# Decay factors by a VectorE scan over rows read back from memory, in place of triangle products and exponentials

## The reference, cut to what matters

```
dt_p = softplus(dt + dt_bias)
A    = -exp(A_log)
dA   = exp(dt_p * A)                  # one factor per sequence, step and head
dtx  = dt_p[..., None] * x
def step(state, inp):
    dA_t, dtx_t, B_t, C_t = inp
    state = state * dA_t[..., None, None] + dtx_t[..., None] * B_t[:, :, None, :]
    y_t = einsum('bhpn,bhn->bhp', state, C_t)
    return (state, y_t)
y = ys + x * D
y = group_norm(y) * norm_weight * silu(gate)
out = y @ out_proj_w.T
```

## Time and profile before

| | |
|---|---|
| median of three runs | 1590.43 us (1589.69 to 1590.87) |
| the profiled execution | 1589.33 us, span 1587.3 us |
| TensorE busy | 1557.8 us, 98% of the span |
| VectorE, ScalarE, GpSimd busy | 1049.1, 852.2, 786.5 us |
| mean granted TensorE clock | 0.996 of full |
| DMA | 80.54 MB, mean 51 GB/s |

### The profile page before, as it was taken

The page is one execution under the profiler, slowest core; times in us unless marked ns, Lnnn a source line. Parts: engine busy times, 40 slices in busy tenths (PEclk is TensorE's granted clock), DMA queues, the critical chain, the costliest instruction groups (busy, mean ns, idle before and its releaser), DMA issues. The chain is left out here.

```text
span 1587.3 us, 32373 instructions
## 1 busy us (share of the span) xinstructions
PE 1557.8 (98%) x12991; PEld 1273.6 (80%) x12991; DVE 1049.1 (66%) x1689; ACT 852.2 (54%) x1420; POOL 786.5 (50%) x747
## 2 busy tenths in 40 slices
PE   8999999999999999999999999999999999999997
PEld 6778888888888888888887888888888888888687
DVE  5877666565657766576877656667565656666566
ACT  4654556555555556555465555555555554545542
POOL 3564545545364554545354463654545463643506
PEclk9999999999999999999999999999999999999999
DMA  6120101111120201111012111202011111103212
GB/s 200 54 60 20 55 21 54 41 41 54 34 61 8 61 28 54 41 41 54 1 55 94 41 54 35 60 8 61 28 54 41 41 54 34 42 20 90 86 41 107
DMA packets 49525, 80.54 MB, mean 51 GB/s; under 512 B 4897, under 2 KB 13601, under 8 KB 49377
## 3 DMA queue, kind: packets, MB, share of 16 engines
q1 hardware_dynamic: 49376, 78.48, 16.0%
HBM read 70.07 MB, written 8.39 MB: 49 GB/s over the span
## 5 line engine op out<-in xcount | busy, mean ns | idle before, releaser
L434 PE MATMUL PS<-xh,wh 128*128 128x512 f32 x1280 | 520.6, 407 | 0.6 <-DVE xl L954 0.6
L434 PE MATMUL PS<-xh,wl 128*128 128x512 f32 x1280 | 500.6, 391 | 0.0
L434 PE MATMUL PS<-xl,wh 128*128 128x512 f32 x1280 | 499.4, 390 | 0.0
L1023 DVE SCALAR_TENSOR_TENSOR cb<-PS,P,cb 128x496 f32<-128x496 f32 (+2 forms) x576 | 412.6, 716 | 129.0 <-ACT cb L755 115.4
L1318 POOL TENSOR_TENSOR wl<-rw,wh 128x512 fp32r<-128x512 f32 x160 | 211.7, 1328 | 187.1 <-ACT wh L706 187.0
L1338 POOL TENSOR_TENSOR ysum<-yq 128x256 f32<-128x256 f32 x128 | 109.1, 852 | 361.6 <-ACT yq L802 361.5
L434 PEld LDWEIGHTS PS<-xh,wl 128*128 128x128 f32 x1280 | 240.7, 188 | 53.5
L434 PEld LDWEIGHTS PS<-xh,wh 128*128 128x128 f32 x1280 | 241.0, 188 | 50.4 <-issue 1.0
L434 PEld LDWEIGHTS PS<-xl,wh 128*128 128x128 f32 x1280 | 241.5, 189 | 44.4
L755 ACT ACTIVATE cb<-PS,P 128x512 f32<-128x512 f32 x192 | 148.3, 773 | 202.7 <-PE PS L434 202.7
L1053 DVE TENSOR_TENSOR big<-Lt,gmt 128x512 f32<-128x512 f32 x128 | 103.0, 846 | 154.3 <-ACT Lt L794 154.3
(11 more groups left out here) (195 smaller groups left out, 2150.0 us busy)
## 6 DMA issues: line engine op xcount, KB each, us to landing
rw<-in_w_in SPq DMA_DIRECT2D x160, 256.0 KB, 2.8
ro<-in_w_out SPq DMA_DIRECT2D x64, 256.0 KB, 2.9
x2s<-acc SPq DMA_DIRECT2D x16, 256.0 KB, 3.3
out_x<-acc SPq DMA_DIRECT2D x16, 256.0 KB, 2.6
acc<-in_x SPq DMA_DIRECT2D x3, 1024.0 KB, 9.7
wh<-x2s SPq DMA_DIRECT2D x8, 256.0 KB, 3.7
wl<-x2s SPq DMA_DIRECT2D x8, 256.0 KB, 4.6
acc<-in_x SPq DMA_DIRECT2D x4, 256.0 KB, 4.6
```

Source lines behind the costliest of these rows:

```text
L434: mm = e.matmul(PS[:, proj_bank(n, m), :], w[:, m, 128 * k:128 * k + 128], v[:, k, a:a + 512], start=(i == 0), stop=(i == 11))
L1023: e.scalar_tensor_tensor(out=cv[:, :, d:32], in0=pv[:, :, 0:32 - d], scalar=P[:, P_CW + 4 * c + 3 - d:P_CW + 4 * c + 4 - d], in1=cv[:, :, ...
```

## The change

The decay over steps s+1 to t is now a running product. The factors exp(av) lie in a row, 32 steps for each head and tile, and a scan along the row computes, at each position, state = max(state * factor, start). `start` (diag) is 1 where the position's step equals the partition's own step s, else 0. The factor at step 0 is set to 0, which ends the run of the head before. So partition s gets 0 before step s, 1 at s, and the product of the factors after it: Lt in one VectorE instruction over 1024 elements.

Each partition of a sequence needs the same row of factors. They are made once for a block, in da (heads on partitions): ScalarE takes the exponential in place, GpSimd zeroes the factors of step 0 (`first_rates`), SyncE stores them into memory by 16 DMAs (`store_rate`), and for every stage reads one row back into 32 partitions each by 4 DMAs (`load_rate`, 128 KB each, into dab). The reads for stage n wait for the stores of the block and for the scan of stage n - 1.

Gone are uf, ah, al, the two transposes of da, `decay_sums`, `expo`, the masked operands on GpSimd. The first decays of a stage are multiplied at m = 8 instead of 9 (in the four TURNED stages the scan is at m = 9 and the product right after it).

```
 (sync)
+            def store_rate(b):
+                sp.wait_ge(rate_zero, b)
+                for r in range(2):
+                    for i in range(2):
+                        for q in range(4):
+                            dst = bass.AP(rates.tensor, b * 32768 + 1024 * q + 256 * (2 * r + i), [[4096, 8], [32, 8], [1, 32]])
+                            a = 128 * i + 32 * q
+                            e.dma_start(dst, da[64 * r:64 * r + 64, a:a + 32]).then_inc(rate_out[b].sem, 16)
+            def load_rate(n):
+                half, g, tb = who(n)
+                b = 2 * half + tb
+                sp.wait_ge(rate_out[b], 15)
+                if n >= 1:
+                    sp.wait_ge(L_ok, n - 1)
+                for q in range(4):
+                    src = bass.AP(rates.tensor, b * 32768 + g * 4096 + 1024 * q, [[0, 32], [1, 1024]])
+                    e.dma_start(dab[32 * q:32 * q + 32, :], src).then_inc(ld_rate.sem, 16)
...
             for u in range(16):
                 for j in range(4):
                     load_o(u, j)
+                    if u % 8 == 0 and j == 2:
+                        store_rate(u // 4)
+                        load_rate(2 * u)
+                if u % 8:
+                    load_rate(2 * u + 1)
                 if u < 15:
                     for m in range(10):
                         load_w(u + 1, m)
+                if u % 8 == 0:
+                    store_rate(u // 4 + 1)
+                    load_rate(2 * u + 1)
+                if u % 8 != 7:
+                    load_rate(2 * u + 2)
 (tensor)
-                pe.wait_ge(d_done, b)
+                pe.wait_ge(d_step, (b, 10))
-                for i, src in enumerate((dr[:, 0:128], dr[:, 128:256], da[:, 0:128], da[:, 128:256])):
-                    mm = e.transpose(PS[:, SEG[0], 128 * i:128 * i + 128], src, ident)
+                for i in range(2):
+                    mm = e.transpose(PS[:, SEG[0], 128 * i:128 * i + 128], dr[:, 128 * i:128 * i + 128], ident)
-            def decay_sums(n):
...
-                    e.matmul(PS[:, SEG[r], :], uf[:, :], avh[:, 512 * r:512 * r + 512], start=True, stop=False)
-                    e.matmul(PS[:, SEG[r], :], uf[:, :], avl[:, 512 * r:512 * r + 512], start=False, stop=True).then_inc(seg_ok.sem, 1)
 (turn_x, second round)
-                    pe.wait_ge(L_ok, (n, 0))
+                    if n in TURNED:
+                        pe.wait_ge(dt_ok, TURNED[n])
 (Y)
-                    pe.wait_ge(L_ok, (n, 1))
 (scalar)
             def dt_first(b):
                 if b >= 1:
                     act.wait_ge(DT_ok, b - 1)
+                    act.wait_ge(rate_out[b - 1], 15)
             def dt_turned(b):
+                act.wait_ge(d_done, b)
+                e.activation(da[:, :], da[:, :], ACT.Exp).then_inc(rate_exp.sem, 1)
                 act.wait_ge(DT_ok, b)
                 e.copy(dtt ...)
-                e.copy(ah ...)
-            def expo(n):
...
-                    e.activation(Lt[:, 512 * r:512 * r + 512], PS[:, SEG[r], :], ACT.Exp).then_inc(L_ok.sem, 1)
 (vector)
-            def dt_turned(b):
...
+            def decays(n):
+                dve.wait_ge(ld_rate, n)
+                if n == 0:
+                    dve.wait_ge(diag_ok)
+                e.tensor_tensor_scan(Lt[:, :], dab[:, :], diag[:, :], 0.0, ALU.mult, ALU.max).then_inc(L_ok.sem, 1)
                     if n == 0 and m == 6:
                         side_inputs()
+                        e.tensor_copy(diag ...)
+                    if m == (9 if n in TURNED else 7):
+                        decays(n)
                     if m == 8:
                         scale_turned(n, 0)
                         scale_turned(n, 1)
-                    if m == 9:
+                    if m == (9 if n in TURNED else 8):
                         decayed(n, 0)
                         decayed(n, 1)
 (gpsimd)
-            def decays(n):
...
+            def first_rates(b):
+                pool.wait_ge(rate_exp, b)
+                e.memset(da[:, :].rearrange("p (a t) -> p a t", t=32)[:, :, 0], 0.0).then_inc(rate_zero.sem, 1)
-                    if m == 6:
-                        decays(n)
+                    if m == 6 and n in TURNED:
+                        first_rates(TURNED[n])
```

More of the change, by code:

```diff
@@ L86, in adaln_attn_ffn_kernel @@
 def adaln_attn_ffn_kernel(nc, x, emb, gin, b2, wbank, biask, w_in, w_dt, w_out, prm, cst, cw4, ctxw,
-                          w_ffn, b_ffn, asg, x2s, out):
+                          w_ffn, b_ffn, asg, x2s, rates, out):
     ctx = ExitStack()
@@ L104, in adaln_attn_ffn_kernel @@
         yl = sb("yl", [128, 2, 512], FR)
-        uf = sb("uf", [128, 128], FR)
-        ah = sb("ah", [128, 8, 64], FR)
-        al = sb("al", [128, 8, 64], FR)
+        dab = sb("dab", [128, 1024])
+        diag = sb("diag", [128, 1024])
         wdh = sb("wdh", [128, 256], FR)
@@ L152, in adaln_attn_ffn_kernel @@
         yss = big[:, 7168:7680].rearrange("p (i t) -> p i t", i=4)
-        pmx = gmt[:, 2, :]
+        pmx, csel = gmt[:, 2, :], dab[0:64, 0:128]
         ident = C[:, C_ID:C_ID + 128]
@@ L240, in adaln_attn_ffn_kernel @@
         d_done, DT_ok = signal("dsp", blocks), signal("DT", blocks)
-        dt_ok, a_hi, a_lo = signal("dtt", blocks), signal("ah", blocks), signal("alo", blocks)
+        dt_ok, rate_exp, rate_zero = signal("dtt", blocks), signal("rx", blocks), signal("rz", blocks)
+        rate_out = [signal(f"ro{b}", range(16), 16) for b in blocks]
+        ld_rate = signal("ld_rate", range(NS), 64)
         w_hi = signal("w_hi", [(u, m) for u in range(16) for m in range(10)])
@@ L250, in adaln_attn_ffn_kernel @@
         xsd_ok = signal("xsd", tiles)
-        av_hi, av_lo = signal("avh", range(NS)), signal("avl", range(NS))
-        seg_ok, L_ok = signal("seg", [(n, r) for n in range(NS) for r in range(2)]), signal("L", [(n, r) for n in range(NS) for r in range(2)])
+        L_ok = signal("L", range(NS))
         T_ok = signal("T", [(n, i) for n in range(NS) for i in (1, 3)])
@@ L581, in stage @@
                         turn_x(n, 0)
[L582 to L585, removed]
+                    if m == 8 and b is not None:
+                        dt_product(b)
                     if m == 9:
@@ L736, in dt_turned @@
                 a = 4 * (b % 2)
-                dt, av = (PS[:, SEG[0], k:k + 256].rearrange("p (i r c) -> p i r c", i=2, r=2) for k in (0, 256))
+                act.wait_ge(d_done, b)
+                e.activation(da[:, :], da[:, :], ACT.Exp).then_inc(rate_exp.sem, 1)
                 act.wait_ge(DT_ok, b)
-                e.copy(dtt[:, a:a + 4, :].rearrange("p (r i) c -> p i r c", r=2), dt).then_inc(dt_ok.sem, 1)
-                e.copy(ah[:, a:a + 4, :].rearrange("p (r i) c -> p i r c", r=2), av).then_inc(a_hi.sem, 1)
+                e.copy(dtt[:, a:a + 4, :].rearrange("p (r i) c -> p i r c", r=2),
+                       PS[:, SEG[0], 0:256].rearrange("p (i r c) -> p i r c", i=2, r=2)).then_inc(dt_ok.sem, 1)
             def evac(n, m):
@@ L1143, in stage @@
                         dt_series(BLOCK_AT[n - 1], *((2, 7), (7, 12))[m - 4])
-                    if m == 6 and n in TURNED:
-                        dt_turned(TURNED[n])
                     if m < 6:
@@ L1318, in split_w_lo @@
                 e.tensor_tensor(wl[:, m, :], rw[:, q % RW, :], f(wh[:, m, :]), ALU.subtract).then_inc(w_lo.sem, 1)
-            def decays(n):
-                half, g, tb = who(n)
-                b = 2 * half + tb
-                pool.wait_ge(dt_ok, b)
-                pool.wait_ge(a_hi, b)
-                pool.wait_ge(a_lo, b)
-                if n >= 1:
-                    pool.wait_ge(O_ok, (n - 1, 3))
-                for src, dst, done in ((ah, avh, av_hi), (al, avl, av_lo)):
-                    e.tensor_tensor(dst.rearrange("p (i h t) -> p i h t", i=4, h=8),
-                                    bc(f(src[:, 4 * tb:4 * tb + 4, 8 * g:8 * g + 8]).rearrange("p i (h o) -> p i h o", o=1), 128, 4, 8, 32),
-                                    bc(C[:, C_V:C_V + 32].rearrange("p (a b t) -> p a b t", a=1, b=1), 128, 4, 8, 32),
-                                    ALU.mult).then_inc(done.sem, 1)
+            def first_rates(b):
+                pool.wait_ge(rate_exp, b)
+                e.memset(da[:, :].rearrange("p (a t) -> p a t", t=32)[:, :, 0], 0.0).then_inc(rate_zero.sem, 1)
             def y_sum(n, i):
@@ L1477 @@
     cst[:, C_ID:C_ID + 128] = np.eye(128)
-    cst[:, C_U:C_U + 128] = same & (p[:, None] > p[None, :])
     t = np.arange(64)
@@ L1507 @@
     x2s = nc.dram_tensor("x2s", (16, 128, 512), F32, kind="Internal").ap()
-    adaln_attn_ffn_kernel(nc, *args, x2s, o)
+    rates = nc.dram_tensor("rates", (4, 8, 4, 1024), F32, kind="Internal").ap()
+    adaln_attn_ffn_kernel(nc, *args, x2s, rates, o)
     r = run_bass_kernel_spmd(nc, [maps], core_ids=[0])
```

43 lines of the change are left out of this document (8 added, 35 removed).

## The result

The changed kernel takes **1605.47 us** (median of four runs, 1605.23 to 1606.21), the kernel before 1590.18 in the four runs beside it: a ratio of 1.0097, with a 95% interval of 1.0085 to 1.011. The prediction on record was 1600, with a range of 1585 to 1617. It is slower by 1%, as in the forecast's own case (number 1 of the list of rivals), and 5.5 us longer than forecast. The profiled execution took 1606.21 us, its span 1604.4, so 17.1 us more span than before.

The account below looks back on a forecast made before the run. TensorE's instruction stream was taken to bound the kernel. From 1589.3 us, minus 31.7 (ordinary stages), plus 31.7 (table stages) and 9.2 (clock) gave 1598.5; with the runs' median 1.1 above the profiled execution, forecast 1600, range 1585 to 1617.

Parts of the forecast that it names:

- number 1 of the list of rivals: The forecast itself: table stages exposed and TensorE's clock falls, 1594 to 1613 us; chance 0.50.
- what goes, in the ordinary stages: 28 ordinary stages lose four TensorE matmuls each (25.5 us) and the waits for the exponential (6.2 us): 31.7 us gained.
- the clock: TensorE's granted clock falls to 0.50 after each of four new idle stretches: 4 x 2.3 = 9.2 us.
- what comes, costs nothing in ordinary stages: In ordinary stages VectorE's scan, covered up to 7.4 us, and SyncE's four reads a stage cost nothing.
- the four chains: Stages 0, 1, 16, 17: uncovered chain from first store to Y, 15.6 us each; Y later by 31.7 us in all.
- The issues: SyncE's sixteen store issues in each table stage, 0.47 us apart, 7.05 us; bounds 0.32 and 0.67 apart.
- The scan: VectorE's scan over 128x1024, taken as two ordinary two-operand passes: 1.4 us; upper bound 7.0 us.
- I follow it to the high part of y and find it just in time: Stages 0 and 16: load_o(n,3) behind the burst delays ScalarE's fourth output cast and dt_first, but still in time for O(n,0).
- the faster one: SyncE issues the small stores much quicker, 0.25 us a step, deciding at 0.34: 1584 us; chance 0.20.
- The worse chain (number 4): Scan at the reciprocal's price, or issues at 0.67 with landings of 3.3 and 4.6: 1615 to 1625 us; chance 0.12.
- The one with no cost of the clock: TensorE keeps its clock, or most of it, in the gaps: no change, 1591 us; chance 0.13.
- VectorE as the bound: VectorE bounds every stage if the scan exceeds 7.4 us; at 8.5 us, 1659 us; chance 0.05.

Follow-up runs that it names:

- e4: The changed kernel with the scan made twice in each of the 28 ordinary stages; 1606.04 us, ratio 1.0098 to the kernel before.
- e3: The changed kernel with four stores of 32 KB instead of sixteen of 8 KB, same bytes; 1578.02 us, ratio 0.9923 to the kernel before.
- e1: The changed kernel with stages 0, 1, 16, 17 reading constants early, not waiting for the stores (decays not the reference's); 1571.54 us.
- e5: The changed kernel with unused filler matmuls on TensorE in its four long gaps; 1602.07 us, ratio 1.007 to the kernel before.
- e7: e3 with series, exponential and zeroed factors one step earlier in stages 1, 16, 17, and stores ahead of some loads; 1564.77 us.
- e9: e8 with the reads of stages 1 and 17 right behind their stores, ahead of both last weight loads; 1563.53 us.
- e8: e7 with stage 16's series, exponential and zeroed factors put back to their former steps; 1565.89 us, ratio 0.9846 to the kernel before.

## Why the prediction came out as it did

**Right: what goes, in the ordinary stages, with its size short by an eighth.** 1.29 us a stage were gained where 31.7 / 28 = 1.13 were forecast: the four matmuls and the wait for the exponential, and 0.16 more. Of these, 0.13 lie inside Y: from the start of Y(n,0) to the next projection it was 1.22 us before and is 1.09 now (stage 5 of both), since the products are made a step earlier and Y(n,1) no longer waits for the second of them. Over the span, with what the clock takes from stages 2 and 18, the 28 stages and the tail give 32.3 where 31.7 - 4.6 = 27.1 follow from the prediction: 5.2 us better.

**Right: what comes, costs nothing in ordinary stages.** No new wait stands there, and e4 doubled the scan for nothing. The cover was there, even for a scan of 2.28 us instead of 1.4.

**Right in place, too small in size: the four chains.** The prediction has 36.3 us for the four table stages (31.7, and the clock of stages 0 and 16 paid in 1 and 17, 4.6); measured are 49.4. From the first store to Y stage 1 took 18.2 us for 15.6, and with the last point below taken out the other three took 18.3 to 18.4: 2.6 to 2.8 too much in each chain, 10.8 in all. The last point below adds 1.9 and 1.3. The first stores, counted from the Y before, went out 0.9 us sooner in sum than forecast (later only in stage 16, by 0.5). That makes the 13.1 that were missing. The terms:

- The issues. 0.47 us apart, from the residual's stores, before their bytes clog the engines. They were about 0.62: 2.2 us more in each chain, the largest of the mis-sized terms. The other bound, 0.67, was the better one. e3 shows what the term weighs.
- The scan. 1.4 from a two-operand pass, measured 2.28. Scan, product and handovers took 3.1 together (140.43 to 143.50) where 2.3 were forecast: 0.8 more a chain. The 0.2 for four handovers had no row behind it; from scan to product it is 0.04, from product to Y 0.05. The sentence on the Trainium skill (DVE: opcode table, instruction layouts, handler registers and perf-mode slots; section 6, Datapath and trigger behaviour) had half throughput, 2.8 us by estimate. The trace agrees with it against my 1.4, and with the 2.8 not quite, as that doubles the fixed part of an instruction too. Two rows of the kernel before, which I had not used, give the parts:

```profile
L1067 DVE TENSOR_TENSOR y<-PS,big 128x512 f32<-128x512 f32 x128 | 87.5, 684 | 16.1 <-PE PS L509 16.1
L1031 DVE TENSOR_TENSOR gmt<-PS,C 128x256 f32<-128x256 f32 x32 | 13.3, 414 | 0.0
```

256 elements more cost 270 ns, 1.05 each, which leaves 0.14 us for the instruction. At half that rate 1024 elements take, by estimate, 2 x 1024 x 1.05 + 144 = 2.30 us; measured are 2.28. That the time by that rule, 1605, is also the measured one is luck: the scan gives 0.9 a chain, 3.5 of the 13.1.

- A path that I followed to the wrong reader. The step "I follow it to the high part of y and find it just in time" failed: load_o(n,3) behind the burst delays the fourth output cast, dt_first behind it, and then the second transposes, which wait for dt_first to have read its PSUM bank (d_max). So Y came 20.3 us after the first store in stage 0 (60.78 to 81.04), not 18.2 as in stage 1. The product that Y needs was done at 79.11 there and at 824.37 in stage 16, so this path alone cost 1.9 and 1.3 us. For these stages the forecast was 5.3 and 4.6, and 9.76 and 9.17 came. e1 shows the path by itself: with the round trip gone it still held TensorE for 9.0 us.

The landings were right: 1.7 us from the last issue for the stores (2.0 forecast), 4.2 for the reads (4.3), 0.4 less together. The stores' place was nearly right: the two stages 1 and 17 cost 15.5 and 15.0, where 10.9 + 2.3 + 2.6 for the longer chain is 15.8.

**Right in kind, a quarter too large: the clock.** 0.50 behind all four gaps, as forecast. The price is to be read from Y's start to the first matmul at the short distance, beside the same stretch behind a filled gap in e5: 1.4 and 1.3 us in stages 1 and 17. In stages 0 and 16, where the second transposes are slow too (1.12 instead of 0.71) and are counted in, it is about 2.5 and 2.1, beside stage 16 of e5. In all 7.3, not 9.2. And that is TensorE's own loss: of the 2.1 of stage 16 only 0.9 came back in e5.

So 36.3 + 13.1 for the table stages and 27.1 + 5.2 for the rest: 49.4 - 32.3 = 17.1, where the forecast had 9.2. The two errors have opposite signs, and it is luck that 5.2 of the 13.1 are hidden in the time. By its own signs the prediction is not wholly right: ordinary stages are 1.29 us shorter and not 0.9 to 1.1, two of the four long idles stand ahead of the second transposes and not of Y, and together they are 46.1 us where near 35 were forecast. Of the rivals, the faster one fell with the stores' 0.62: it needed 0.34 a step. But e3 shows that its mechanism decides: with fewer steps instead of quicker ones the change is a gain of 0.8%. The worse chain (number 4) came near in its issues, 0.62 for 0.67, but neither in its scan (2.28 for 7.0) nor in its landings. The one with no cost of the clock fell with e5, VectorE as the bound with e4.

What stays open: why the stores of stage 0 landed 1.7 us later in e5, and what decides whether a short gap costs the clock.

## What to carry to other kernels

A round trip through memory on the path of a chain is priced by the number of its DMA issues first: sixteen small stores took 9.8 us of a queue, four with the same bytes 2.6. Count the issues, merge them by laying out the memory for it, and put what others wait for ahead of them in the queue. Follow each load that a burst is put ahead of to all its readers, through every instruction queued behind the one that waits for it, and not only to the first.

## What the hardware showed that I had not expected

- A store from 64 partitions takes 0.57 us of SyncE's queue with 8 KB and 0.62 with 32 KB (medians): the price is by the piece.
- The scan takes 2280 to 2293 ns for 128x1024 in all 32 stages of the kernel after, where nothing of GpSimd runs beside it. In e1, stage 1, it ran beside GpSimd's splits and took 3.25 us:

```profile
118.66 3.25 DVE L1009 TENSOR_TENSOR_SCAN Lt<-dab,diag 128x1024 f32<-128x1024 f32 x1
120.07 4.59 POOL L1322 TENSOR_TENSOR wl<-rw,wh 128x512 fp32r<-128x512 f32 x2 [0.31 <-ACT wh L718]
```

- Gaps of 2.07 + 0.98 us and of 1.23 + 0.98 us cost TensorE its clock for some microseconds (e7 and e9, stage 1), one of 1.50 + 0.98 us did not (e7, stage 17). A short gap can cost more than a long one: behind that of e7 the distance to Y(2,0) was 47.64 for 43.69, so 3.0 us beside the 0.98. A chain shortened by 1.6 us can give nearly all of it back in this way, as in e8.
- Even the single idle of 1.66 us ahead of the first transposes in stage 16 of the kernel after (808.17) was followed by a lower clock, while the same 1.66 in stage 0 was not; there the time lost went into the gap of 5.80 us behind it. The window behind it:

```profile
810.00:812.00 2.00, 2.00 (x6) 1.57 (x5) 2.00 (x4) 1.67 (x3) 0.00 (x0) 0.50 0.08 12
```

- VectorE's product took 3.25 us for two beside two splits of GpSimd, against 1.29 for two alone.
